# The first masks ahead of a product input on VectorE, and a code shift of TensorE ahead of the half product

## What is computed

```python
x = x + _L0_conv_ref(_gn(x), L0_conv_weight)          # 3x3 convolution, 256 -> 256 channels
x = x + _L1_conv_ref(_gn(x), qkv_w, proj_w, bn_...)   # linear attention in 4x4 windows

# in _L1_conv_ref, per window of 16 tokens and head of 8 channels:
qkv = jnp.einsum('nchw,oc->nohw', xw, qkv_w)
pooled = _avg_pool5(qkv)                              # a second set of heads, from 5x5 averages
msq = jnp.concatenate([qkv, pooled], axis=1)
q, k = relu(q), relu(k); v = [v, 1]
kv = jnp.einsum('ngld,nglm->ngdm', k, v)
out = jnp.einsum('ngld,ngdm->nglm', q, kv)
out = out[..., :-1] / (out[..., -1:] + 1e-15)
y = jnp.einsum('nchw,oc->nohw', out, proj_w)          # then batch norm
```

## Time and profile before

| | us |
|---|---|
| median of 3 runs (2402.37 to 2407.95) | 2404.32 |
| the profiled execution | 2404.27 |
| its span, first to last instruction | 2402.4 |
| TensorE busy, matmuls | 2345.2 |
| TensorE busy, weight loads (beside matmuls) | 2137.7 |
| VectorE busy | 1688.7 |
| ScalarE busy | 1418.7 |
| GpSimd busy | 1039.8 |
| granted TensorE clock, mean | 0.996 |

### The profile page before, as it was taken

One profiled execution on the slowest core, in us unless ns is written; L12 is line 12 of the kernel. 1 busy time (PEld: TensorE's weight loads), 2 busy tenths in 40 slices (PEclk: granted clock), 3 DMA queues, 4 the chain that ended last, 5 costly groups with the idle time before them and its releaser, 6 DMA issues.

```text
span 2402.4 us, 110819 instructions
## 1 busy us (share of the span) xinstructions
PE 2345.2 (98%) x49224; PEld 2137.7 (89%) x49224; DVE 1688.7 (70%) x3207; ACT 1418.7 (59%) x3659; POOL 1039.8 (43%) x1597
## 2 busy tenths in 40 slices
PE   7999999999999999999999999999999999999998
PEld 7988899888998889988899888998889988898887
DVE  9876758767587675876658766687766867665674
ACT  2158851588516884178831788327882278813886
POOL 0036650366404663046630566206661156612666
PEclk9999999999999999999999999999999999999999
DMA  4000010000200002000010000200001000000000
GB/s 172 1 2 16 20 66 10 2 19 16 75 1 3 19 16 75 1 6 19 16 71 1 6 20 16 71 1 10 16 20 67 1 9 20 21 9 2 16 16 25
DMA packets 39106, 58.31 MB, mean 24 GB/s; under 512 B 4704, under 2 KB 36064, under 8 KB 36832
## 3 DMA queue, kind: packets, MB, share of 16 engines
q1 hardware_dynamic: 38880, 55.27, 6.5%
HBM read 29.57 MB, written 25.69 MB: 23 GB/s over the span
## 4 chain that ended last, share of the span: by engine, by line
PE 92%; DVE 5%; issue 2%; ACT 1%; DMA 0%; SPq 0%; POOL 0%; POOLq 0%; ACTq 0%; DVEq 0%
PE ps L353 33%; PE ps L428 15%; PE ps L372 12%; PE ps L417 10%; PE ps L403 8%; PE ps L381 6%; PE ps L392 4%; PE ps L438 3%; DVE xh L1018 1%; ACT ve L667 1%; DVE kv_part L1031 1%; DMA xs<-w_conv 0%; DVE kvm L1058 0%; DVE dp L926 0%; DVE ao L1049 0%
## 5 line engine op out<-in xcount | busy, mean ns | idle before, releaser
L1247 POOL TENSOR_TENSOR ve<-vpraw,vmask 128x1024 f32<-128x1024 f32 x200 | 386.0, 1930 | 1193.2 <-ACT vpraw L678 1193.1
L353 PE MATMUL ps<-dp,wc 128*128 128x392 f32 x4608 | 840.1, 341 | 0.6 <-DVE dp L926 0.6
L353 PEld LDWEIGHTS ps<-dp,wc 128*128 128x128 f32 x4608 | 816.0, 188 | 4.5 <-issue 1.6
L428 PEld LDWEIGHTS ps<-at,wp 128*128 128x128 f32 x3200 | 388.4, 192 | 51.0 <-issue 25.8
L428 PE MATMUL ps<-at,wp 128*128 128x128 f32 (+1 forms) x3200 | 418.3, 279 | 1.0 <-ACT yb L723 1.0
L648 ACT CAST dp<-dt 128x896 fp32r<-128x896 f32 x128 | 120.9, 945 | 448.9 <-PE ps L353 356.6
L372 PE MATMUL ps<-wkv,xt 128*128 128x512 f32 x1200 | 324.4, 405 | 0.6 <-issue 0.5
L417 PEld LDWEIGHTS ps<-kvm,qs 64*32 64x32 f32 x25088 | 232.5, 105 | 99.0 <-issue 97.7
L667 ACT ACTIVATE ve<-ps,vmask 128x256 f32<-128x256 f32 x800 | 314.3, 491 | 0.0
L1026 DVE TENSOR_TENSOR xt<-xh,xt 128x256 fp32r<-128x256 f32 x200 | 104.1, 520 | 270.8 <-ACT xt L655 270.7
L417 PE MATMUL ps<-kvm,qs 64*32 64x36 f32 x25088 | 258.2, 204 | 25.7 <-issue 24.3
(11 more groups left out here) (88 smaller groups left out, 2876.6 us busy)
## 6 DMA issues: line engine op xcount, KB each, us to landing
out<-xs SPq DMA_DIRECT2D x224, 112.0 KB, 1.8
xs<-x SPq DMA_DIRECT2D x14, 1344.0 KB, 8.2
xs<-x SPq DMA_DIRECT2D x14, 224.0 KB, 2.7
xs<-w_conv SPq DMA_DIRECT2D x2, 1152.0 KB, 12.2
xs<-x SPq DMA_DIRECT2D x2, 896.0 KB, 6.5
xs<-x SPq DMA_DIRECT2D x2, 672.0 KB, 7.7
kvm<-w_kv SPq DMA_DIRECT2D x1, 512.0 KB, 13.6
wp<-w_proj SPq DMA_DIRECT2D x4, 128.0 KB, 9.9
```

Of the source, the lines that this page charges most:

```text
L353: last = nc.tensor.matmul(ps[:, conv_bank(v, mt), 0:CONV_N], wc[:, part_w, k, kt * TAPS + dy, mt * P:(mt + 1) * P], dp[:, kk % 2, part_d, ...
L428: last = nc.tensor.matmul(ps[:, BANK_Q, mt * TT:mt * TT + n], wp[:, q, mt * P:(mt + 1) * P], at[:, q, e, 0:n], start=(q == 0), stop=(q == ...
L1247: nc.gpsimd.tensor_tensor(ve[:, t % 2, :, 1].rearrange("p e (n m) -> p e n m", m=DIM + 1)[:, :, :, 0:DIM], vpraw[:].rearrange("p (n m) -> ...
```

## The change

Three edits:

- On VectorE, in `first_chunk`, the input of product v + 5 moves from ahead of the addition of product v + 3 to behind the first tile's masks, and the row statistics that belonged to that addition move there too, as `row_stats(v + 3, 0)`. The statistics of all other additions stay where they were.
- On TensorE, a new shift, `at_slot(SLOT_HALF)` with 7, in turn 0 between `keys_times_values` and the half product.
- The shift to slot 80 ahead of the loop stays for the last image alone, which has no half product.

No instruction other than the shift's is added or taken away, and ScalarE, GpSimd and the DMAs keep their order.

```diff
-SLOT_LEAD, SLOT_FIRST, SLOT_LOOP, SLOT_OUT = 160, 68, 80, (68, 44)
+SLOT_LEAD, SLOT_FIRST, SLOT_HALF, SLOT_LOOP, SLOT_OUT = 160, 68, 7, 80, (68, 44)
...
                 if half and s == 0:
+                    at_slot(SLOT_HALF)
                     pe.wait_ge(qraw_ready, pairs - 1)
                     product(*half)
...
-                at_slot(SLOT_LOOP)
+                if v is None:
+                    at_slot(SLOT_LOOP)
...
-                if kk == len(PRODUCTS) - 1:
-                    dve.wait_ge(conv_added, 2 * v + mt + 5)
-                    for half in range(2):
-                        o = c * (CONV_H * W) + half * CONV_N
-                        last = nc.vector.bn_stats(st1[:, mt, 2 * c + half, :], xs[:, img % 2, mt, o:o + CONV_N])
-                    last.then_inc(st1_done, 1)
+                if kk == len(PRODUCTS) - 1 and not (c == 0 and mt == 0 and img):
+                    row_stats(v, mt)
+
+            def row_stats(v, mt):
+
+                img, c = divmod(v // len(PRODUCTS), CONV_CHUNKS)
+                dve.wait_ge(conv_added, 2 * v + mt + 5)
+                for half in range(2):
+                    o = c * (CONV_H * W) + half * CONV_N
+                    last = nc.vector.bn_stats(st1[:, mt, 2 * c + half, :], xs[:, img % 2, mt, o:o + CONV_N])
+                last.then_inc(st1_done, 1)
...
                 kv_low_part(b, 1)
-                product_inputs(v + 5)
                 add_product(v + 3, 0)
                 mask(b, 0, 0)
                 mask(b, 0, 1)
+                row_stats(v + 3, 0)
+                product_inputs(v + 5)
```

## The result

| | median | runs | ratio to before, 95% interval |
|---|---|---|---|
| before | 2405.45 us | 6 | |
| the changed kernel | 2421.59 us | 6 | 1.0071 (1.0055 to 1.0087) |

The change makes the kernel slower by 16 us, where 7 were forecast: the direction was right, and the size was less than half of what was measured. The profiled execution of the changed kernel is its slowest, 2429.49 us (span 2427.6); the other five lie between 2421.2 and 2423.2.

The account below looks back on a forecast made before the run. TensorE, busy 98% of the span, was taken to bound the kernel. The half product starting 1.04 us later, masks' gain included, in seven images gave 7.3 us: 2404.3 + 7.3 = 2411.6 us, range 2403 to 2416.

Parts of the forecast that it names:

- What bounds the kernel: TensorE, busy 98% of the span: a change pays only where it removes TensorE's idle time and costs where it adds some.
- the counting of slots: TensorE's code in blocks of 256 slots: a boundary after attend's 83rd load, the half product starting at slot 220.
- The masks' gain: At the hand-over from convolution to attention, earlier masks on VectorE let attend start sooner: 0.72 us gained per image, in seven.
- the block's price: Ahead of the half product, the new shift waits for its code, usable 3.3 us after attend's boundary; product 1.04 us later.
- What is queued behind the masks: VectorE's tile 3 normalisation comes 0.88 us late; by VectorE alone the q of the pair begins 0.44 us later.
- The earlier trace with 3.85: Last image before the change: the loop's shift into the next block ended 3.85 us after the boundary; taken as upper bound.
- The first: Rival: code fetch is hidden at the new shift, VectorE's late addition decides; 3.1 us lost, 2407.4 us; chance 0.20.
- the second: Rival: fetch hidden and VectorE's chain closes up, so the masks' 5.0 us stay whole, 2399.3 us; chance 0.08.
- The third: Rival: the loop's first pass changes, its 1.97 us stall going; up to 13 us back, 2398.6 us; chance 0.10.

## Why the prediction was right in direction and short in size

**What bounds the kernel, and the counting of slots: right.** The losses and gains that I could place are idle time of TensorE or its clock, and the boundaries fell where the count put them: in the run with the shift in its own block, attend breaks off after its 83rd load.

**The masks' gain: right.** 0.72 us per image forecast, 0.77 measured ahead of attend (5.4 us over seven hand-overs in the changed kernel and in the run with the masks alone). What the earlier attend does to the code behind it was missed; see the block's price.

**What is queued behind the masks: right, and shown.** Forecast as 0.44 us per image by VectorE alone; the run with the masks alone has turn 0 longer by 1.16 and attend earlier by 0.77, so 0.39 per hand-over. In the changed kernel it was covered, as I wrote: VectorE waited 2.79 us for the half product.

**The block's price: right mechanism, short in size. This is the step that failed for the total.** I took 3.3 us from boundary to use, between 2.9 and 3.85, and so a product that starts 1.04 us later than before. In the third image the boundary is crossed at 755.61 + 83/128 x 1.28 = 756.44 and the product starts at 760.36: 3.92 us. Over the seven images the product's first load starts 4.0 to 4.5 us behind the 83rd load of attend, 4.2 in the mean, and 1.87 us later than before. The DMA view of 754 to 764 us has the two pieces of the third image:

```profile
GB/s 66 0 0 0 0 0 0 0 0 0 0 0 0 0 0 66 0 0 0 0 0 0 0 0 0 0 0 66 0 0 0 0 0 0 0 0 0 0 0 0
```

The packet starts in the slice from 757.75, 1.3 to 1.6 us after the boundary where I had 0.8 to 1.1, and the product follows 2.4 to 2.6 us behind that where I had 2.1 to 2.3. The first piece has grown because of the masks. With the shift alone, attend at its old place, the packet starts 0.8 to 1.3 us behind the 83rd load, as the rows of before had it, and the product 3.6 to 4.1 (3.8 in the mean) behind that load. With the masks forward attend comes 0.77 us earlier but reaches the boundary before the block there has arrived: the 84th load comes up to 0.65 us late, and the packet starts 1.2 to 1.8 us behind the 83rd. So 0.5 us of the masks' gain is lost again at the block boundary, an interaction that the prediction put at nothing. The earlier trace rows with 3.85 were the nearest to the measured price, and I averaged them away.

Without the clock, turn 0 is 84.2 to 84.3 us (the runs with the eight matmuls) against 66.0, or 2.6 per image, where I had 1.04 + 0.72 = 1.76. That is 6 us of the 9 by which the forecast was short.

**The term that is missing: the clock.** The account ends with the product's start, and puts what follows at nothing. That step failed too. In five or six of seven images the granted clock fell to 0.5 behind an idle time of 1.9 to 2.5 us, and the product's loads took 1.4 to 1.6 us longer. In turn 0 that is 8 to 9 us (92.3 and 93.7 against 84.2 and 84.3). The Trainium skill ("TensorE: Matmul & The Clock Gate", Part 1 on the clock gate) says that TensorE's clock is at 1.2 GHz when the engine has been idle and at 2.4 when it is busy; the rows of this case agree on the two levels, and I should have asked of any idle time that I add what the clock does behind it. The trace of before would have warned, too: the clock was lowered behind the loop's stall in three images. In the third, 767 to 771 us, the granted clock is 0.57:

```profile
767.00:771.00 4.00, 3.51 (x88) 3.07 (x88) 2.96 (x5) 0.69 (x2) 0.00 (x0) 0.57 0.01 4
```

**But the clock is not what the total lost.** Turns 1 and 2 became shorter by 2.3 to 4.9 us, with the clock lowered there in one image or none instead of three; with the fall in turn 0 prevented, it came back there. The total moved by 2 us, which the intervals can't tell from nothing. So the account of the medians' 16 us is: 7 x 2.6 = 18 for the block, less 5 for the masks, and some 2 for the clock on balance, which makes 15. The last microsecond is less than executions differ by in turns 3 to 23. The terms are worked out from single executions, so the split between the clock and those turns isn't settled.

**The rivals.** The first (the fetch is hidden) and the second fell with the 2.55 us branch. The third asked whether the loop's stall would change with the shift: it didn't (turn 2 takes 10.2 to 11.9 us after, 10.2 to 11.7 before), but its guess that as much as 13 us lie there was sound: with the product input in turn 0 the stall went, for 7 to 10 us in turns 1 and 2.

## What to carry to other kernels

Where code is laid out by hand, ask of each block boundary how long the instructions behind the last one take: here a block could be used 3.6 to 4.6 us after the boundary before it, 256 quick instructions take 1.2 us, and only slow ones (the product's 36 take 3.15 us) cover the rest. A step that is pulled forward in one engine's list pushes what it overtakes in front of something else; ask which of the overtaken steps feeds another engine, and put the ones that feed nobody soon (here the statistics and the product input) behind it. What reaches a boundary earlier also waits longer there: of the 0.77 us that attend gained, 0.5 went to the fetch. A total that doesn't move when a local cost goes means that the cost has moved: look for where else it now falls.

## What the runs showed of the hardware

- A branch into a block of code that isn't there held TensorE's queue for 2.2 to 2.8 us; one within the block took 178 ns. The block could be used 2.4 to 3.0 us after its 16 KB packet had started.
- The granted clock fell to half behind an idle time of 2.25 to 2.5 us in five of seven images of one execution, and in three images of another behind stalls of 1.6 to 1.9 us. It stayed up behind 2.37 us in the first of them, so the idle time alone doesn't decide. With TensorE kept at work it didn't fall at that place.
- A wait of 0.63 us for another engine at a block boundary removed a stall of 1.97 us in the next block in six of seven images, so that a kernel became faster by an added delay. In all twelve profiles the stall was absent where TensorE reached `pooled` 2.8 us or more after the start of the preceding packet (13 cases) and there where it came within 2.4 us (71 cases); the next packet came 0.4 to 1.5 us after `pooled` began in the one case and 3.8 to 4.4 in the other. The cause is open.
